# Layer 0 scan: which of the sixteen states' inputs ScalarE scales and TensorE turns, and which are made with diagonals of B

## The chip, the cores and the metric

The kernel runs on one core of a Trainium2 chip. The metric is the device time of one launch, in microseconds; it is given as the median of several runs. All four layers of the model are in this one launch. The change lies in layer 0 alone.

## What is computed

The model has four layers over an image tensor of shape (4, 48, 48, 128). Layer 0 is a two-dimensional selective state-space block. Cut to what matters here:

```python
# per image b, direction k (4: rows, columns, and both backwards), channel d (256), state n (16)
x_dbl = einsum('bkdl,kcd->bkcl', xs, x_proj_w)          # 8 dt rows, 16 B rows, 16 C rows
dt = softplus(einsum('bkrl,kdr->bkdl', dts_r, dt_proj_w) + dt_proj_b)
def step(h, inp):                                       # over the 2304 positions l
    dA = exp(dt_l[..., None] * A)
    h = h * dA + (dt_l * u_l)[..., None] * B_l[:, :, None, :]
    y = einsum('bkdn,bkn->bkd', h, C_l)
    return h, y
```

The result is the sum of the four directions, normalised, gated and projected. Layer 1 is a deformable convolution, layer 2 linear attention with experts, layer 3 causal attention and spectral filters; they are not touched.

## The kernel before

The scan of an image runs over the four directions, each cut into 6 pieces of 384 positions: 24 chunks per image, named g. Within a chunk it runs over the 16 states, so that there are 384 steps s with n = s % 16 and g = s // 16. Positions lie along the free axis, and the 256 channels are two halves of 128 partitions, which one scan instruction handles together.

For each step, the engines do this:

- ScalarE makes the decays exp(dt * A) with two instructions (`decays`, line 500), two steps ahead of the scan. There are four decay buffers.
- The input dt * u * B of the state is made in PSUM by `make_input` on TensorE, one step ahead of the scan, in one of two PSUM places. B varies along the positions, which are on the free axis, so it cannot be a per-partition factor there. There are two ways around it. A *straight* state uses `diagonal` on VectorE (line 556), which multiplies the identity with B to get three 128x128 diagonals, and six matmuls (line 408) of the turned dt * u with these. A *turned* state uses `turned_input` on ScalarE (line 490), which multiplies dt * u in its turned form by B as a per-partition scale, three instructions, and six transposes (line 406) back. `TURNED` lists the turned states. Diagonals are made two steps ahead and have three buffers; turned inputs are made three steps ahead and have two buffers (xT), so that one waits until the input of the turned state two before it has been made.
- VectorE scans (`scan`, line 579). A scan waits for its decays, its input and its carry.
- GpSimd multiplies the states with the C row (line 647) and then writes the carry columns for the step three ahead (`carry`, line 636, or a memset on line 634 in a direction's first chunk).
- TensorE turns the product and sums it over the states into y in PSUM (`sum_states`, line 419), three steps behind.

Beside this, in fixed slots of a chunk, the next chunk is projected (`project`). On TensorE: the rows of dt, B and C in slot 0 (line 361), the two halves of the dt projection in slots 2 and 5 (line 377), the turning of B in slot 8 (line 369) and of dt * u in slots 11 and 13 (line 389). ScalarE copies the rows in slot 1 (line 460), does the softplus in slots 3 and 6 (lines 470 to 474), and copies B and the turned dt * u later (lines 464 and 480). VectorE finishes dt after scans 4 and 7 (line 549). GpSimd multiplies dt * u after the product of state 7 (line 619). For directions 1 and 3 the rows and dt * u go through a view with x and y exchanged.

The finished y of a chunk is taken out of PSUM in the next one. In the first two directions ScalarE copies it, after the softplus of slot 3 (`keep_y`, line 506). In the other two VectorE adds it, after scan 2 (`add_y`, line 586). State 0 of the following chunk may be summed (S(0), the first of line 419 in a chunk) only after that.

Every engine works in the order that is written here. In step s TensorE does `make_input(s + 1)`, then `sum_states(s - 3)`, then `project`; ScalarE does `turned_input(s + 3)`, `decays(s + 2)`, `project`, `keep_y`; VectorE does `diagonal(s + 2)`, `scan(s)`, `project`, `add_y`. `make_input(s)` also waits until scan s - 2 has freed its PSUM place.

Of the kernel before, what the change touches and what calls it, by code (L numbers as in the profile page):

```python
# [70 lines left out]
NCS, NDC, NHC = 6, 4, 4  # L71
RX = 2 * RC + 6
X2_AT = BANK - RC - 4
TURNED = (2, 5, 7, 10, 12, 15)


def layer0(nc, x_in, w, x_out, c_rows):
    with ExitStack() as ctx:
# [107 lines left out]
        with nc.Fori(0, NB) as b:  # L186
# [107 lines left out]
            with nc.Block() as block:  # L294
# [13 lines left out]

                turned = [s for s in range(NSTEP) if s % NS in TURNED]
                straight = [s for s in range(NSTEP) if s % NS not in TURNED]  # L310
                rank = {s: i for own in (turned, straight) for i, s in enumerate(own)}
# [14 lines left out]
                def half(h):  # L326

                    return slice(2 + h * (RC + 2), 2 + h * (RC + 2) + RC)
# [26 lines left out]
                def _(pe):  # L355
# [36 lines left out]
                    def make_input(s):  # L392
                        n, g = s % NS, s // NS
                        if n == 0:
                            pe.wait_ge(s_tc, 2 * g + 2)
                        if n in TURNED:
                            pe.wait_ge(s_xT, rank[s] + 1)
# [4 lines left out]
                        for h in range(2):  # L402
                            for t in range(LB):
                                o = 2 * BANK * (s % 2) + X2_AT + half(h).start + t * P
                                if n in TURNED:
                                    mm = pe.transpose(ps[:, o:o + P], xT[:, rank[s] % 2, t, h * P:(h + 1) * P], ident[:])  # L406
# [46 lines left out]
                def _(act):  # L453
# [29 lines left out]
                    def turned_input(s):  # L483
                        n, g, i = s % NS, s // NS, rank[s]
                        act.wait_ge(s_bt, g + 1)
                        act.wait_ge(s_tc, 2 * g + 2)
                        if i >= 2:
                            act.wait_ge(s_x2, turned[i - 2] + 1)
                        for t in range(LB):
                            ins = act.activation(xT[:, i % 2, t, :], dtuT[:, g % 2, t, :], ACT.Copy, scale=BT[:, g % 2, t, n:n + 1])  # L490
                        ins.then_inc(s_xT, 1)
# [38 lines left out]
                    for s in range(3):  # L530
                        if s % NS in TURNED:
                            turned_input(s)
                    for s in range(NSTEP):
                        if s + 3 < NSTEP and (s + 3) % NS in TURNED:
                            turned_input(s + 3)
# [2161 lines left out]
```

## Time and profile before

| | us |
|---|---|
| median of 3 runs | 7712.57 |
| lowest and highest run | 7707.59, 7712.93 |
| span of the profiled execution | 7975.8 |
| TensorE busy in it | 7187.8 (90%) |
| VectorE busy | 5972.5 (75%) |
| ScalarE busy | 4078.3 (51%) |
| GpSimd busy | 3659.8 (46%) |

The profile is of one execution. Its span, from the first to the last instruction, is the only time known of that execution, and it is longer than the median. Layer 0 takes about the first half of it. The rows below are read so: an instruction's start and duration, then in square brackets how long its engine had been idle before it and what ended that. The durations of two neighbours on an engine can overlap, so the distance from start to start is what an instruction takes of its engine's queue.

### The profile page before, as it was taken

How to read it: one execution, taken by the hardware profiler on the slowest of the kernel's cores; microseconds unless marked ns; L12 is line 12 of the kernel's file. 1: busy time of each engine (PE TensorE's matmuls, PEld its weight loads, DVE VectorE, ACT ScalarE, POOL GpSimd, SP SyncE). 2: the span in 40 equal slices, each digit the busy share in tenths (PEclk: the TensorE clock that was granted, in tenths of full speed). 3: DMA queues.
4: the chain of work that ended last, by engine and by line, in shares of the span. 5: the costliest groups of instructions: out<-in, count | busy, mean ns of one | idle time of the engine just before them, and what ended most of it. 6: DMA issues, size and time to landing. Idle time of an engine off the chain costs nothing. (4 is left out here: it accounts for less than half of the span.)

```text
span 7975.8 us, 170513 instructions
## 1 busy us (share of the span) xinstructions
PE 7187.8 (90%) x62522; PEld 6186.6 (78%) x62522; DVE 5972.5 (75%) x9085; ACT 4078.3 (51%) x8541; POOL 3659.8 (46%) x4037
## 2 busy tenths in 40 slices
PE   8999899998999989999756788879988999999999
PEld 6888778886788867888546666645667989989999
DVE  7999889997899978999644555545556767767677
ACT  5888668885688757888311222224543222222222
POOL 5888658885688847888355555410000000000000
PEclk9999999999999999999878899889998999999999
DMA  2333223332233322333366555400003434434343
GB/s 66 90 93 93 75 64 92 93 90 68 74 90 93 92 58 83 90 94 90 109 174 171 164 160 152 119 4 3 0 6 95 125 116 125 125 116 128 113 129 108
DMA packets 590364, 763.42 MB, mean 96 GB/s; under 512 B 51703, under 2 KB 527896, under 8 KB 587585
## 3 DMA queue, kind: packets, MB, share of 16 engines
q1 hardware_dynamic: 537921, 585.72, 25.8%
q0 software_dynamic: 51840, 169.91, 7.5%
q8 instruction: 348, 5.70, 0.3%
q14 instruction: 255, 2.09, 0.1%
HBM read 721.77 MB, written 33.66 MB: 95 GB/s over the span
## 5 line engine op out<-in xcount | busy, mean ns | idle before, releaser
L647 POOL TENSOR_TENSOR l_arena<-l_arena 128x768 f32<-128x768 f32 x1536 | 2591.3, 1688 | 449.1 <-DVE l_arena L579 443.6
L579 DVE TENSOR_TENSOR_SCAN l_arena<-l_arena,psum 128x772 f32<-128x772 f32 x1536 | 2664.5, 1751 | 176.6 <-PE psum L406 72.5
L500 ACT ACTIVATE l_arena<-l_arena,l_A 128x384 f32<-128x384 f32 x3072 | 1643.7, 604 | 38.2 <-DVE l_arena L579 32.7
L408 PE MATMUL psum<-l_arena 128*128 128x128 f32 x11520 | 1499.3, 280 | 46.8 <-DVE l_arena L579 43.0
L408 PEld LDWEIGHTS psum<-l_arena 128*128 128x128 f32 x11520 | 1367.4, 192 | 170.5 <-issue 146.7
L419 PE MATMUL psum<-l_ident,l_arena 128*128 128x128 f32 x9216 | 1257.6, 273 | 50.6 <-ACT l_yT L506 41.7
L419 PEld LDWEIGHTS psum<-l_ident,l_arena 128*128 128x128 f32 x9216 | 1055.2, 141 | 60.2 <-POOL l_arena L647 60.2
L2269 POOL TENSOR_TENSOR st_mab<-st_xr 128x384 f32<-128x384 f32 x8 | 7.8, 1000 | 2053.1 <-DVE st_xr L2259 2053.1
L1211 POOL DMA_INDIRECT l_G<-neighbours,l_idx x648 | 621.2, 959 | 650.2 <-PE psum L1259 301.0
L490 ACT ACTIVATE l_arena<-l_arena,l_BT 128x256 f32<-128x256 f32 x1728 | 747.0, 496 | 7.5
L2544 ACT ACTIVATE st_own_s<-psum 128x384 f32<-128x384 f32 x256 | 125.7, 491 | 1092.5 <-PE psum L2381 1092.5
L1259 PE MATMUL psum<-l_ident,l_G 128*128 128x128 f32 x2592 | 361.8, 301 | 181.2 <-ACT l_val L1384 109.8
L2381 PE MATMUL psum<-st_FS,st_xt 128*128 128x128 f16 x6912 | 518.0, 219 | 4.4 <-DMA st_FS<-filter_sums 4.4
L556 DVE TENSOR_TENSOR l_arena<-psum,l_BT 128x384 f32<-128x384 f32 x960 | 510.8, 532 | 0.0
L1259 PEld LDWEIGHTS psum<-l_ident,l_G 128*128 128x128 f32 x2592 | 333.5, 157 | 212.6 <-issue 198.4
L406 PEld LDWEIGHTS psum<-l_ident,l_arena 128*128 128x128 f32 x3456 | 380.5, 140 | 143.8 <-issue 141.3
L406 PE MATMUL psum<-l_ident,l_arena 128*128 128x128 f32 x3456 | 486.9, 277 | 2.8 <-DVE l_arena L579 2.8
L2401 PE MATMUL psum<-st_Uc,st_Wm 128*128 128x128 f32 (+1 forms) x2560 | 448.6, 306 | 6.4 <-DVE st_Uc L2521 6.4
L2381 PEld LDWEIGHTS psum<-st_FS,st_xt 128*128 128x128 f16 x6912 | 434.7, 97 | 21.1 <-DMA st_FS<-filter_sums 4.8
L1054 DVE TENSOR_TENSOR l_G<-l_G,psum 128x1536 f32<-128x1536 f32 (+1 forms) x144 | 365.5, 2547 | 84.2 <-DMA l_G<-neighbours,l_idx 73.9
L2371 PE MATMUL psum<-st_F,st_xt 128*128 128x128 f16 x4608 | 427.4, 219 | 0.0
L2401 PEld LDWEIGHTS psum<-st_Uc,st_Wm 128*128 128x128 f32 x2560 | 351.4, 191 | 7.5 <-DVE st_Uc L2521 7.5
(436 smaller groups left out, 11291.5 us busy)
## 6 DMA issues: line engine op xcount, KB each, us to landing
l_arena<-c_rows SPq DMA_DIRECT2D x1536, 192.0 KB, 3.1
st_FS<-filter_sums SPq DMA_DIRECT2D x128, 1155.0 KB, 9.2
st_F<-filter_parts SPq DMA_DIRECT2D x128, 320.5 KB, 7.2
neighbours<-l_xt SPq DMA_DIRECT2D x256, 72.0 KB
st_mab<-in_st_mp SPq DMA_DIRECT2D x68, 256.0 KB, 9.5
st_mab<-in_st_mm SPq DMA_DIRECT2D x68, 256.0 KB, 6.2
l_G<-neighbours,l_idx POOLq DMA_INDIRECT x648
l_arena<-in_x SPq DMA_DIRECT2D x4, 1152.0 KB, 5.2
```

What stands on the lines that cost most here:

```text
L406: mm = pe.transpose(ps[:, o:o + P], xT[:, rank[s] % 2, t, h * P:(h + 1) * P], ident[:])
L408: mm = pe.matmul(ps[:, o:o + P], dtuT[:, g % 2, t, h * P:(h + 1) * P], diagB[:, rank[s] % 3, t, :], start=True, stop=True)
L419: mm = pe.matmul(y_ps[:, t, h * P:(h + 1) * P], hC[:, s % NHC, h, t * P:(t + 1) * P], ident[:], start=(n == 0 and h == 0 and t % 2 == 0), ...
L490: ins = act.activation(xT[:, i % 2, t, :], dtuT[:, g % 2, t, :], ACT.Copy, scale=BT[:, g % 2, t, n:n + 1])
L500: act.activation(decay[:, s % NDC, half(h)], dtv[:, g % 2, h, :], ACT.Exp, scale=A[:, g // NRC, h, n:n + 1]).then_inc(s_exp, 1)
L556: dve.tensor_tensor(diagB[:, i % 3], ident_ps.unsqueeze(1).broadcast_to([P, LB, P]), BT[:, g % 2, :, n:n + 1].broadcast_to([P, LB, P]), AL ...
L579: dve.tensor_tensor_scan(hbuf[:, n, run], decay[:, s % NDC, run], x2_ps[s % 2][:, run], 0.0, ALU.mult, ALU.add).then_inc(s_scan, 1)
L647: pool.tensor_tensor(hC[:, s % NHC], halves(hbuf[:, s % NS, :]), Cs[:, s % NCS, :].unsqueeze(1).broadcast_to([P, 2, RC]), ALU.mult).then_i ...
L1211: pool.indirect_dma_start(out=G[:, g, 4 * k:4 * k + 4, :].rearrange("p q c -> p (q c)"), out_offset=None, in_=tables[b], in_offset=bass.In ...
L1259: mm = pe.matmul(bank(i % 2, P * a, P * (a + 1)), G[:, g, 4 * k + q, :], ident[:], start=(q == 0), stop=(q == 3), is_transpose=True, skip_ ...
L2381: mm = pe.matmul(ps[:, at + i * P:at + (i + 1) * P], xt[:, xpart, x0 + LB - 1 - i, :], FS[:, r, fpart, z, three, shift + i * P:shift + (i ...
L2401: mm = pe.matmul(ps[:, o:o + hi - lo], Wm[:, r, z, m, :], src[:, lo - c * RC:hi - c * RC], start=False, stop=False, skip_group_check=True)
```

## The change

One line: the list of turned states goes from six to eight, and not by adding two. States 4, 8, 11 and 13 become turned, and 7 and 12 become straight; 2, 5, 10 and 15 stay turned.

```diff
@@ -71,7 +71,7 @@
 NCS, NDC, NHC = 6, 4, 4
 RX = 2 * RC + 6
 X2_AT = BANK - RC - 4
-TURNED = (2, 5, 7, 10, 12, 15)
+TURNED = (2, 4, 5, 8, 10, 11, 13, 15)
```

What this does to the order is seen on the engines. On TensorE, in a chunk from the first half of the dt projection (line 377) to the input of state 8; the rows of line 419 are the sums of states 0 to 3 of this chunk. Before:

```order
L377 MATMUL psum<-l_arena,l_dtp_w 128x384
L408 MATMUL psum<-l_arena 128x128 x6
L419 MATMUL psum<-l_ident,l_arena 128x128 x6
L406 MATMUL psum<-l_ident,l_arena 128x128 x6
L419 MATMUL psum<-l_ident,l_arena 128x128 x6
L408 MATMUL psum<-l_arena 128x128 x6
L419 MATMUL psum<-l_ident,l_arena 128x128 x6
L377 MATMUL psum<-l_arena,l_dtp_w 128x384
L406 MATMUL psum<-l_ident,l_arena 128x128 x6
L419 MATMUL psum<-l_ident,l_arena 128x128 x6
L408 MATMUL psum<-l_arena 128x128 x6
```

The same place on TensorE in the changed kernel:

```order
L377 MATMUL psum<-l_arena,l_dtp_w 128x384
L406 MATMUL psum<-l_ident,l_arena 128x128 x6
L419 MATMUL psum<-l_ident,l_arena 128x128 x6
L406 MATMUL psum<-l_ident,l_arena 128x128 x6
L419 MATMUL psum<-l_ident,l_arena 128x128 x6
L408 MATMUL psum<-l_arena 128x128 x6
L419 MATMUL psum<-l_ident,l_arena 128x128 x6
L377 MATMUL psum<-l_arena,l_dtp_w 128x384
L408 MATMUL psum<-l_arena 128x128 x6
L419 MATMUL psum<-l_ident,l_arena 128x128 x6
L406 MATMUL psum<-l_ident,l_arena 128x128 x6
```

The input of state 4, behind the first line 377, is now turned; that of state 7, behind the second, is now made with diagonals; that of state 8 is turned.

On VectorE, in a chunk from its second dt update (line 549, after scan 7) to scan 13. Before:

```order
L549 SCALAR_TENSOR_TENSOR l_arena<-psum,l_arena 128x384
L579 SCALAR_TENSOR_TENSOR l_arena<-l_arena,psum 128x772
L556 TENSOR_TENSOR l_arena<-psum,l_BT 128x384
L579 SCALAR_TENSOR_TENSOR l_arena<-l_arena,psum 128x772 x2
L556 TENSOR_TENSOR l_arena<-psum,l_BT 128x384
L579 SCALAR_TENSOR_TENSOR l_arena<-l_arena,psum 128x772
L556 TENSOR_TENSOR l_arena<-psum,l_BT 128x384
L579 SCALAR_TENSOR_TENSOR l_arena<-l_arena,psum 128x772 x2
```

The same place on VectorE in the changed kernel:

```order
L549 SCALAR_TENSOR_TENSOR l_arena<-psum,l_arena 128x384
L579 SCALAR_TENSOR_TENSOR l_arena<-l_arena,psum 128x772 x2
L556 TENSOR_TENSOR l_arena<-psum,l_BT 128x384
L579 SCALAR_TENSOR_TENSOR l_arena<-l_arena,psum 128x772 x2
L556 TENSOR_TENSOR l_arena<-psum,l_BT 128x384
L579 SCALAR_TENSOR_TENSOR l_arena<-l_arena,psum 128x772 x2
```

The diagonals of states 11 and 13 are gone and that of state 12 has come, before scan 10. Scans 8 and 9 now stand back to back.

## Rows read from the trace of the kernel before

**Rows 1.** The page's costliest groups: instruction, count, busy us, mean ns, idle before.

```profile
L408 PE MATMUL psum<-l_arena 128*128 128x128 f32 x11520 | 1499.3, 280 | 46.8 <-DVE l_arena L579 43.0
...
L490 ACT ACTIVATE l_arena<-l_arena,l_BT 128x256 f32<-128x256 f32 x1728 | 747.0, 496 | 7.5
...
L556 DVE TENSOR_TENSOR l_arena<-psum,l_BT 128x384 f32<-128x384 f32 x960 | 510.8, 532 | 0.0
...
L406 PE MATMUL psum<-l_ident,l_arena 128*128 128x128 f32 x3456 | 486.9, 277 | 2.8 <-DVE l_arena L579 2.8
```

**Rows 2.** Window of chunk 5: length, busy PE, PEld, DVE, ACT, POOL, granted clock, DMA.

```profile
268.47:304.07 35.60, 34.64 (x272) 29.88 (x270) 32.47 (x29) 28.85 (x62) 30.50 (x34) 1.00 0.33 90
```

**Rows 3.** Timeline of VectorE, chunk 10: start us, us, instruction, idle before.

```profile
446.75 1.76 DVE L579 TENSOR_TENSOR_SCAN l_arena<-l_arena,psum 128x772 f32<-128x772 f32 x1 [1.84 <-POOL l_arena L636]
...
451.78 1.76 DVE L579 TENSOR_TENSOR_SCAN l_arena<-l_arena,psum 128x772 f32<-128x772 f32 x1 [0.82 <-PE psum L408]
...
454.23 1.76 DVE L579 TENSOR_TENSOR_SCAN l_arena<-l_arena,psum 128x772 f32<-128x772 f32 x1 [0.24 <-ACT l_arena L500]
...
458.52 1.76 DVE L579 TENSOR_TENSOR_SCAN l_arena<-l_arena,psum 128x772 f32<-128x772 f32 x1
460.20 0.53 DVE L549 SCALAR_TENSOR_TENSOR l_arena<-psum,l_arena 128x384 f32<-128x384 f32 x1
...
466.09 0.53 DVE L556 TENSOR_TENSOR l_arena<-psum,l_BT 128x384 f32<-128x384 f32 x1
466.54 1.75 DVE L579 TENSOR_TENSOR_SCAN l_arena<-l_arena,psum 128x772 f32<-128x772 f32 x1
...
481.09 1.76 DVE L579 TENSOR_TENSOR_SCAN l_arena<-l_arena,psum 128x772 f32<-128x772 f32 x1 [0.58 <-PE psum L406]
```

**Rows 4.** Timeline of TensorE, start of chunk 10.

```profile
443.00 2.75 PE L361 MATMUL psum<-l_xc,l_xp_w 128*40 128x384 f32 x4
...
449.97 1.60 PE L408 MATMUL psum<-l_arena 128*128 128x128 f32 x12
452.52 0.85 PE L419 MATMUL psum<-l_ident,l_arena 128*128 128x128 f32 x6 [0.95 <-ACT l_yT L506]
...
456.60 0.91 PE L377 MATMUL psum<-l_arena,l_dtp_w 9*128 9x384 f32 x2
457.44 0.88 PE L406 MATMUL psum<-l_ident,l_arena 128*128 128x128 f32 x6
```

**Rows 5.** Timeline of ScalarE, start of chunk 10.

```profile
445.78 0.49 ACT L460 ACTIVATE l_arena<-psum 40x384 f32<-40x384 f32 x1 [3.53 <-PE psum L361]
446.17 1.30 ACT L490 ACTIVATE l_arena<-l_arena,l_BT 128x256 f32<-128x256 f32 x3
447.36 2.12 ACT L500 ACTIVATE l_arena<-l_arena,l_A 128x384 f32<-128x384 f32 x4
450.07 0.49 ACT L470 ACTIVATE l_arena<-psum 128x384 f32<-128x384 f32 x1 [0.58 <-PE psum L377]
```

**Rows 6.** Timeline of GpSimd, chunk 10, and one row of chunk 15.

```profile
460.36 1.69 POOL L647 TENSOR_TENSOR l_arena<-l_arena 128x768 f32<-128x768 f32 x1 [0.36 <-DVE l_arena L579]
...
462.13 2.39 POOL L619 TENSOR_TENSOR l_arena<-l_arena,l_xc 128x384 f32<-128x384 f32 x2
...
466.09 0.20 POOL L636 COPY l_arena<-l_arena 128x2 f32<-128x2 f32 x1
...
634.23 1.97 POOL L619 TENSOR_TENSOR l_arena<-l_arena,l_xc 128x384 f32<-128x384 f32 x2
```

**Rows 7.** Timeline of TensorE and VectorE, chunk 15: inputs 6, 7; scans 5, 7.

```profile
626.16 1.58 PE L408 MATMUL psum<-l_arena 128*128 128x128 f32 x12 [0.59 <-DVE l_arena L579]
...
629.16 0.87 PE L406 MATMUL psum<-l_ident,l_arena 128*128 128x128 f32 x6
...
626.38 1.75 DVE L579 TENSOR_TENSOR_SCAN l_arena<-l_arena,psum 128x772 f32<-128x772 f32 x1
...
630.62 1.75 DVE L579 TENSOR_TENSOR_SCAN l_arena<-l_arena,psum 128x772 f32<-128x772 f32 x1
```

## The prediction, made before the changed kernel ran

> **What bounds the kernel now.** I read the page's costliest groups first [rows 1]. The change touches three kinds of work in the layer 0 scan: the diagonals of B on VectorE (line 556), the B-scaled inputs on ScalarE (line 490) and TensorE's making of the scan input (lines 408 and 406). The window of one whole chunk [rows 2] says how full each engine is: in 35.60 us TensorE is busy 34.64, VectorE 32.47, ScalarE 28.85, GpSimd 30.50. No engine has much room, so busy time decides nothing. The timelines of one chunk [rows 3 to 6] have to be walked.
>
> I call the 24 runs of 16 states per image chunks 0 to 23. Chunk 10 is shown; its state 2 is scanned at 446.75 and that of chunk 11 at 481.09 [rows 3], and a chunk is measured here from its scan 2 to the next. I write x(n) for the input of state n in PSUM, and S(n) for the six transposes of line 419 that add state n to y. Three facts carry the argument.
>
> First, TensorE works in program order, and around the start of a chunk it, not VectorE, sets the pace. The row projection (2.75 us) runs from 443.00, and x(2) comes only after it [rows 4]. In chunk 10, S(0) starts at 452.52 after 0.95 us of idle that ScalarE's copy of y (line 506) ends. From there TensorE runs through x(5), S(1), x(6), S(2), the second dt projection at 456.60 and x(7) at 457.44 [rows 4].
>
> Second, the price of an input as the scan sees it. Straight (line 408, 12 instructions): x(4) starts at 449.97 and its scan at 451.78, so 1.81 us [rows 3, 4]. Turned (line 406, 6 instructions): x(7) starts at 457.44 and its scan at 458.52, so 1.08 us [rows 3, 4]. The difference is 0.73 us.
>
> Third, a diagonal costs VectorE 0.45 us of its queue, from 466.09 to the scan at 466.54 [rows 3]; the 0.53 of its own row overlaps the next instruction.
>
> **The change, part by part.** States 4, 8, 11 and 13 become turned, states 7 and 12 straight. Per chunk that is two diagonals fewer on VectorE (2 x 0.45 = 0.90 us), two more triples on ScalarE (2 x 1.20 = 2.4 us, by the 1.20 from 446.17 to 447.36 that one takes in the queue [rows 5]), and on TensorE 2 x 0.66 less. If all the VectorE saving reached the end, 96 chunks would give 86 us. It does not, state by state:
>
> State 4, turned. Its diagonal stood before scan 2, which waits 1.84 us for the projection [rows 3], or 0.58 in a chunk with the short one. So taking it away gains nothing. x(4) is ready 0.73 earlier, but S(0) behind it waits for the copy of y at 452.52, and that copy hangs on the first dt projection and the softplus on ScalarE, which do not move. So scan 5 stays at 454.23 and the gain of x(4) is lost. ScalarE's added triple for state 4 stands before the wait of 3.53 us at 445.78 and is hidden. The triple for state 5 must now wait until x(2) is made, at 446.17 + 0.4, because there are two xT buffers. That is covered by the 0.58 idle before 450.07 [rows 5]. If that cover were short, the dt softplus, the copy of y, S(0) and all behind them would be late.
>
> State 7, straight. This is the loss. x(7) starts at 457.44 as before, right behind the second dt projection, but takes 1.81 instead of 1.08. Scan 7 moves from 458.52 to 459.25: **+0.73**. The diagonals that move there (8 away before scan 6, 7 added before scan 5) are no help, since VectorE is waiting for TensorE: without the wait, scan 7 could start at about 458.3. This holds in the 12 chunks with the copy of y (1 to 12). In the chunks with the add of y on VectorE (13 to 22) TensorE waits 0.59 for scan 4 before x(6) at 626.16, x(7) starts at 629.16 and its scan at 630.62 [rows 7]. It becomes 629.16 + 1.81 = 630.97: **+0.35**.
>
> States 8, 11, 13 turned and 12 straight, from scan 7 on. VectorE sets the pace there, and between scans 7 and 15 it loses diagonals 11 and 13 and gains 12: **-0.45**. x(9) stays straight with one diagonal less around it. It is ready 0.23 + 1.81 = 2.04 us after scan 7 ends (0.23 from scan 4's end at 625.93, the start 626.38 of [rows 7] less 0.45, to 626.16), against 2.12 that the dt update and scan 8 take. So it fits, with 0.08 to spare.
>
> GpSimd, untouched, is late next. Scan n needs the carry that GpSimd writes after the product of state n-3. After scan 7 its queue holds delta x u (line 619): 2.39 us in chunks 5 to 10 and 17 to 22, where it writes through a turned view, 1.97 in the others [rows 6]. The carry for scan 11 ends at 466.29, 6.09 us after scan 7's end at 460.20. Scan 11 started 6.34 after, and now would start 5.89 after [rows 3, 6]. The trace shows no wait of VectorE on GpSimd that is certain; the way over is between 0 (466.29 itself) and 0.25 (since 6.34 was no wait). ScalarE to TensorE and VectorE to GpSimd take 0.05 to 0.2 (460.20 to 460.36 [rows 3, 6]), so I take 0.1. That gives 6.19 - 5.89 = **+0.30**, with bounds 0.20 and 0.45, in those 12 chunks; in the short ones 0.4 us less, thus nothing (at most 0.06).
>
> The Trainium skill has a rule against this reading. "Perfetto Trace Analysis", section Identifying the Most-Contended Engine, says that the engine with the highest occupancy is to be relieved first, and that TensorE's room is to be judged by LDWEIGHTS busy time, not by matmul busy time. By that rule VectorE is the bound, with 32.47 us against 29.88 of weight loads [rows 2], and the whole VectorE saving would arrive. The rows above disagree at the start of a chunk, where VectorE idles.
>
> **The sum**, per image: 12 chunks x (0.73 - 0.45) = +3.4; 10 chunks x (0.35 - 0.45) = -1.0; GpSimd 12 x 0.30 = +3.6; chunk 0, which has neither copy nor add of y, about -0.25 and chunk 23, which projects nothing and is held by straight inputs and the last add, about -0.1. Together +5.6 us, over four images **+22 us**. Against the profiled span that is 7975.8 to 7998. The span is 263 us (3.4%) above the median of 7712.57, and nothing shows where. The terms are lengths of queued instructions at a granted clock of 1.00 [rows 2], so I carry them over unchanged: 7735 us, 0.29% slower. With GpSimd's bounds: 12 x 4 x 0.20 = 9.6 to 12 x 4 x 0.45 = 21.6, plus 2.4 for the short chunks, in place of 14.4. The sum is then 18 to 32, time 7730 to 7745.
>
> **The rivals.**
>
> A. VectorE is the bound throughout, the whole 0.90 us per chunk arrives: 7712.6 - 86 = 7626. For it: VectorE is busy 32.47 of 35.60, and for most of a chunk its rows are back to back. Against it: the waits before scans 2, 4 and 5 [rows 3]. This is also what the skill's rule would give.
>
> B, the other side. TensorE catches up before x(7), so that straight 7 costs nothing, and only diagonals 11 and 13 less 12 count, -0.45 in every chunk: -43. With GpSimd's 14 it is 7684. It is decided by whether x(7) starts before about 456.5 in chunk 10; that takes S(0) about 0.9 earlier than 452.52. For it: x(4) ends 0.7 earlier. Against it: the wait that holds S(0) ended with line 506, not with TensorE.
>
> C. Both signs cancel, since unprofiled waits are shorter than profiled ones: the loss at scan 7 shrinks to about half (0.37 and 0.18), and per image that is 12 x (-0.08) - 10 x 0.27 + 3.6 - 0.35 = -0.4. Time about 7711, band 7697 to 7727.
>
> D. ScalarE is late in the copy of y. The cover is 0.58 - 0.4 = 0.18 us. If a triple that waits costs 0.4 more than I took, 12 x 4 x 0.4 = 19 us come on top: 7754; with late inputs for 8, 10, 11 too, up to 7770. For it: 2.4 us more on an engine of 28.85. Against it: it idles 3.53, 0.58 and more in each chunk [rows 5].
>
> **How the numbers follow.** Forecast 0.58, A 0.04, B 0.14, C 0.13, D 0.11. The predicted time is the forecast's, 7735. Left out are A and B with 0.18; the range then runs from C's lower end to just under D's upper one: 7697 to 7765. A difference under 0.2%, 15.4 us, is about what a measurement of this kernel cannot tell from none. Faster by more: A and B, 0.18. Within: C and the thin lower edge of the forecast, 0.16. Slower: 0.66.
>
> **What would show each step.** In the changed trace: scan 7 of chunk 10 waits for line 408 and starts 3.0 us after scan 6, where it was 2.2; scan 5 stays 7.48 us behind scan 2; scan 4 comes 0.7 earlier; the idle before S(0) grows from 0.95 to about 1.7; scan 11 has a wait on line 636 of about 0.3 in chunks 5 to 10 and 17 to 22, and none elsewhere. Chunk 10 gets about 0.6 longer (34.34 to 34.9), one like chunk 2 about 0.3 longer, one like 15 0.1 shorter. Line 556 has 768 instructions, line 490 has 2304. I am wrong if scan 7 does not wait for TensorE, or if the copy of y moves.

## The result, and the profile after

| | before | after |
|---|---|---|
| median, us | 7712.75 | 7791.76 |
| lowest and highest of 4 runs each | 7707.59, 7713.07 | 7790.40, 7796.82 |
| span of the profiled execution | 7975.8 | 7790.3 |
| first and last statistics of layer 0 (line 196), start us | 15.6, 2949.0 | 15.5, 3006.0 |

The ratio is 1.0109, with a 95% interval from 1.0094 to 1.0123: 1.1% slower, 79 us. The forecast was 7735, the range 7697 to 7765. The sign was right, the size was not: of 79 us only 22 had been foreseen.

The page of the changed kernel, its span, the busy times, the granted clock in 40 slices, and the groups that answer to [rows 1]:

```profile
span 7790.3 us, 168593 instructions
...
PE 7053.1 (91%) x61370; PEld 6041.7 (78%) x61370; DVE 5897.6 (76%) x8893; ACT 4312.5 (55%) x9117; POOL 3655.8 (47%) x4037
...
L408 PE MATMUL psum<-l_arena 128*128 128x128 f32 x9216 | 1212.5, 282 | 116.4 <-DVE l_arena L579 95.4
...
L490 ACT ACTIVATE l_arena<-l_arena,l_BT 128x256 f32<-128x256 f32 x2304 | 997.3, 496 | 56.6 <-PE psum L406 49.1
...
L406 PE MATMUL psum<-l_ident,l_arena 128*128 128x128 f32 x4608 | 668.8, 283 | 24.3 <-DVE l_arena L579 23.7
...
L556 DVE TENSOR_TENSOR l_arena<-psum,l_BT 128x384 f32<-128x384 f32 x768 | 409.2, 533 | 0.0
```

The work moved as the diff says: 192 diagonals fewer, 576 scalings more, 1152 transposes more, 2304 straight matmuls fewer. VectorE's busy time fell by 75 us, TensorE's by 135, and the kernel is 79 us slower. The line for 406 has its mean up from 277 [rows 1] to 283 ns. A transpose has no reason to take longer, so the clock has to be looked at. That comes below.

The profiled span of before is not a guide to the result. Of the 263 us by which it exceeds the median, 255 lay in layer 1, as the gathers of its line 1211 show, first in the trace of before, then of after (count, ns min/median/max, first and last start):

```profile
L1211 POOL DMA_INDIRECT l_G<-neighbours,l_idx x648: 943/949/2733, 4006.7 to 5131.9; - x162
```

```profile
L1211 POOL DMA_INDIRECT l_G<-neighbours,l_idx x648: 942/949/2792, 4082.1 to 4952.0; - x162
```

They took 1125 us in that one execution of before and 870 in after. When they start, after is 75 us behind. So nearly the whole loss is in layer 0, and there the profile of before is a sound base.

### The profile page after: what moved, and what is told of

Same layout as the page of the kernel before. It is cut to its first block and busy times, and to the rows that moved or that the text cites. A ratio compares the mean times of both kernels' runs of the same rounds, so it can differ in the third digit from the quotient of the medians.

```text
span 7790.3 us, 168593 instructions
## 1 busy us (share of the span) xinstructions
PE 7053.1 (91%) x61370; PEld 6041.7 (78%) x61370; DVE 5897.6 (76%) x8893; ACT 4312.5 (55%) x9117; POOL 3655.8 (47%) x4037
## 3 DMA queue, kind: packets, MB, share of 16 engines
q1 hardware_dynamic: 537921, 585.72, 25.6%
## 5 line engine op out<-in xcount | busy, mean ns | idle before, releaser
L419 PE MATMUL psum<-l_ident,l_arena 128*128 128x128 f32 x9216 | 1290.2, 277 | 87.4 <-ACT l_yT L506 80.4
L408 PE MATMUL psum<-l_arena 128*128 128x128 f32 x9216 | 1212.5, 282 | 116.4 <-DVE l_arena L579 95.4
L408 PEld LDWEIGHTS psum<-l_arena 128*128 128x128 f32 x9216 | 1100.3, 193 | 258.4 <-issue 245.6
L419 PEld LDWEIGHTS psum<-l_ident,l_arena 128*128 128x128 f32 x9216 | 1082.5, 144 | 100.2 <-POOL l_arena L647 97.4
L490 ACT ACTIVATE l_arena<-l_arena,l_BT 128x256 f32<-128x256 f32 x2304 | 997.3, 496 | 56.6 <-PE psum L406 49.1
L406 PE MATMUL psum<-l_ident,l_arena 128*128 128x128 f32 x4608 | 668.8, 283 | 24.3 <-DVE l_arena L579 23.7
L406 PEld LDWEIGHTS psum<-l_ident,l_arena 128*128 128x128 f32 x4608 | 529.0, 144 | 174.7 <-issue 167.9
L556 DVE TENSOR_TENSOR l_arena<-psum,l_BT 128x384 f32<-128x384 f32 x768 | 409.2, 533 | 0.0
L1259 PE MATMUL psum<-l_ident,l_G 128*128 128x128 f32 x2592 | 314.8, 281 | 69.9 <-DVE l_G L1054 41.8
L1259 PEld LDWEIGHTS psum<-l_ident,l_G 128*128 128x128 f32 x2592 | 299.5, 145 | 92.4 <-DVE l_G L1054 47.9
```

What stands on the lines that cost most here:

```text
L408: mm = pe.matmul(ps[:, o:o + P], dtuT[:, g % 2, t, h * P:(h + 1) * P], diagB[:, rank[s] % 3, t, :], start=True, stop=True)
L419: mm = pe.matmul(y_ps[:, t, h * P:(h + 1) * P], hC[:, s % NHC, h, t * P:(t + 1) * P], ident[:], start=(n == 0 and h == 0 and t % 2 == 0), ...
L1259: mm = pe.matmul(bank(i % 2, P * a, P * (a + 1)), G[:, g, 4 * k + q, :], ident[:], start=(q == 0), stop=(q == 3), is_transpose=True, skip_ ...
```

## Where the 79 us are: one chunk length at a time

VectorE's second dt update (line 549, after scan 7) comes once in a chunk. The distance from one to the next, worked out from the starts of line 549 in the traces, is the length of a chunk, and from an image's first to its last is called its scan block here. The first image:

| us, from chunk to chunk | 1 to 2 | 3 to 4 | 6 to 7 | 8 to 9 | 10 to 11 | 16 to 17 | 19 to 20 |
|---|---|---|---|---|---|---|---|
| before | 34.34 | 34.33 | 35.89 | 35.60 | 34.33 | 35.65 | 35.65 |
| after | 34.61 | 36.53 | 37.72 | 37.65 | 36.61 | 35.56 | 35.90 |
| after, with transposes in the gap (`e5_fill`, below) | 34.61 | 34.88 | 36.03 | 36.18 | 34.93 | 35.56 | 35.89 |

The scan blocks of the four images sum to 3181.4 us before and 3259.3 after: +77.8, which is the result but for about 1 us. Some chunks behave as forecast (1 to 2: +0.27, forecast +0.28; 16 to 17: -0.09, forecast -0.10). The chunks into 4 to 11, in the later images 1 as well, are 1.4 to 1.7 us longer on top of that.

In such a chunk, chunk 9 of the changed kernel, VectorE's timeline reads so (start us, us, instruction, idle before and what ended it):

```profile
421.78 1.76 DVE L579 TENSOR_TENSOR_SCAN l_arena<-l_arena,psum 128x772 f32<-128x772 f32 x1 [2.29 <-POOL l_arena L636]
...
426.08 1.76 DVE L579 TENSOR_TENSOR_SCAN l_arena<-l_arena,psum 128x772 f32<-128x772 f32 x1
427.76 0.53 DVE L549 SCALAR_TENSOR_TENSOR l_arena<-psum,l_arena 128x384 f32<-128x384 f32 x1
...
430.55 1.76 DVE L579 TENSOR_TENSOR_SCAN l_arena<-l_arena,psum 128x772 f32<-128x772 f32 x1 [1.79 <-PE psum L406]
432.69 1.76 DVE L579 TENSOR_TENSOR_SCAN l_arena<-l_arena,psum 128x772 f32<-128x772 f32 x1 [0.38 <-PE psum L408]
...
435.72 1.76 DVE L579 TENSOR_TENSOR_SCAN l_arena<-l_arena,psum 128x772 f32<-128x772 f32 x1 [0.82 <-PE psum L408]
437.39 0.53 DVE L549 SCALAR_TENSOR_TENSOR l_arena<-psum,l_arena 128x384 f32<-128x384 f32 x1
...
443.61 1.76 DVE L579 TENSOR_TENSOR_SCAN l_arena<-l_arena,psum 128x772 f32<-128x772 f32 x1 [0.24 <-POOL l_arena L636]
```

Scan 4 comes 4.30 us behind scan 2, against 5.03 before [rows 3], so the gain of x(4) is there. Scan 5 then waits 1.79 us for its transposes and comes 8.77 behind scan 2, where 7.48 was forecast and measured before. Scan 7 comes 3.03 behind scan 6, with a wait of 0.82 for line 408, as forecast. Why x(5) is late stands on TensorE, in the same chunk:

```profile
424.16 0.91 PE L377 MATMUL psum<-l_arena,l_dtp_w 9*128 9x384 f32 x2
425.00 0.87 PE L406 MATMUL psum<-l_ident,l_arena 128*128 128x128 f32 x6
427.55 1.51 PE L419 MATMUL psum<-l_ident,l_arena 128*128 128x128 f32 x6 [1.68 <-ACT l_yT L506]
428.86 1.49 PE L406 MATMUL psum<-l_ident,l_arena 128*128 128x128 f32 x6
430.13 1.01 PE L419 MATMUL psum<-l_ident,l_arena 128*128 128x128 f32 x6
430.98 1.50 PE L408 MATMUL psum<-l_arena 128*128 128x128 f32 x12
```

x(4) is done early, and TensorE then idles 1.68 us for the copy of y, not 0.95 [rows 4]. The six transposes S(0) behind it take 1.51 us in place of 0.85, and those of x(5) 1.49. The windows of these stretches show what TensorE's clock did (length, busy PE, PEld, DVE, ACT, POOL, granted clock, DMA share, GB/s):

```profile
420.70:425.80 5.10, 5.10 (x39) 4.22 (x38) 3.78 (x3) 4.48 (x10) 3.00 (x5) 1.00 0.27 85
425.80:427.55 1.75, 0.07 (x2) 0.03 (x1) 1.66 (x2) 1.72 (x4) 1.63 (x2) 0.87 0.29 94
427.55:428.86 1.31, 1.31 (x7) 1.31 (x8) 1.20 (x3) 1.31 (x4) 0.00 (x0) 0.50 0.33 67
428.86:430.13 1.27, 1.27 (x7) 1.27 (x7) 0.00 (x0) 1.27 (x4) 0.89 (x1) 0.50 0.55 109
430.13:430.98 0.85, 0.85 (x7) 0.85 (x7) 0.43 (x1) 0.85 (x2) 0.85 (x2) 0.77 0.08 23
430.98:433.90 2.92, 2.92 (x22) 2.21 (x20) 2.54 (x2) 0.65 (x2) 1.58 (x2) 1.00 0.20 67
```

The granted clock was 1.00, fell during this idle, stood at 0.50, which is 1.2 of 2.4 GHz, for S(0) and x(5), and came back during S(1). Over 92 to 930 us it was 1.00 before and is 0.98 after:

```profile
92.00:930.00 838.00, 813.86 (x6423) 713.84 (x6422) 784.58 (x695) 677.56 (x1435) 730.46 (x816) 1.00 0.32 91
```

```profile
92.00:930.00 838.00, 783.61 (x6000) 677.10 (x6000) 751.00 (x637) 723.51 (x1557) 711.96 (x800) 0.98 0.30 90
```

In 35 of the 48 chunks with a copy of y the clock falls (8 in the first image, 9 in each other): there the distance from the first to the second dt update is 9.57 to 9.87 us, in the other 13 it is 8.19 or 8.20. Those 13 have the same idle. In chunk 2 of the changed kernel, TensorE's row for S(0) and the windows of the idle and of what follows read:

```profile
169.34 0.84 PE L419 MATMUL psum<-l_ident,l_arena 128*128 128x128 f32 x6 [1.68 <-ACT l_yT L506]
```

```profile
165.80:169.30 3.50, 1.86 (x10) 0.93 (x8) 3.41 (x3) 3.36 (x8) 3.24 (x4) 1.00 0.33 102
169.30:170.70 1.40, 1.36 (x13) 1.40 (x14) 1.24 (x3) 1.40 (x4) 0.34 (x1) 1.00 0.26 88
```

So the longer idle makes a fall possible and does not force it. The Trainium skill tells of a like case in "TensorE: Matmul & The Clock Gate", section A second HAM failure mode: psum-queue depth-cycling: short idles between groups of matmuls, not one long stop, let the clock go back and forth between its two levels. The trace agrees, with 0.50 behind 1.68 us of idle.

## The experiments

The theory after the trace: turning state 4 lengthens TensorE's idle ahead of S(0) by 0.73 us, the clock falls at it, and that is some 57 of the 79 us; the terms of the forecast are the rest. The rivals: the loss is from the fuller ScalarE, or from state 7 and GpSimd at more than their price, and the clock only shows it; or the clock falls because TensorE has less to do in the whole chunk, and not because of this one idle. The runs were made in three sets, each with runs of before on the same chip: e1, e2 and e4 against 7709.6 us, e5 to e8 against 7708.9, e9 and e10 against 7704.94.

| label | turned states, other edit | us | ratio to before, 95% interval |
|---|---|---|---|
| e2_four_straight | 2, 5, 8, 10, 11, 13, 15 | 7725.25 | 1.0020 (1.0010 to 1.0029) |
| e1_four_only | 2, 4, 5, 7, 10, 12, 15 | 7734.48 | 1.0030 (1.0019 to 1.0042) |
| e4_seven_for_four | 2, 5, 7, 8, 10, 11, 13, 15 | 7665.29 | 0.9942 (0.9926 to 0.9959) |
| e5_fill | as after, 12 more transposes in the idle | 7726.85 | 1.0025 (1.0014 to 1.0036) |
| e7_after_copy_first | as after, copy of y ahead of the softplus | 7661.07 | 0.9935 (0.9918 to 0.9951) |
| e6_best_copy_first | as e4, copy of y ahead of the softplus | 7627.78 | 0.9893 (0.9877 to 0.9910) |
| e8_split_du | as e6, dt * u of GpSimd in two parts | 7617.85 | 0.9883 (0.9866 to 0.9899) |
| e10_before_copy_first | as before, copy of y ahead of the softplus | 7681.27 | 0.9969 (0.9956 to 0.9982) |
| e9_nine | as e8, and 4 | 7615.90 | 0.9882 (0.9864 to 0.9900) |

### State 4 straight again

```diff
-TURNED = (2, 4, 5, 8, 10, 11, 13, 15)
+TURNED = (2, 5, 8, 10, 11, 13, 15)
```

> The changed kernel with state 4 straight again (turned: 2, 5, 8, 10, 11, 13, 15). Clock theory: in the changed kernel, turning state 4 lengthens TensorE's idle before S(0) from 0.95 to 1.68 us, and the granted clock falls to half there in 8 or 9 of the 12 chunks with the copy of y. With state 4 straight the idle is 0.95 again and the clock stays full, while straight state 7 still costs 0.73 and 0.35. Sum per image: 12 x 0.28 - 10 x 0.1 + 12 x 0.2 - 0.3 = 4.5 us, so 7731 us (7722 to 7740). Rival, ScalarE theory: the loss comes from the extra ScalarE work or its order in the other states; then it stays near 7780 (over 7760). Rival, state 7 is dearer than thought: also near 7780, with full clock.

Measured 7725.25: 16 us over its own before, where after is 79 over, so 63 us are back. TensorE at S(0), chunk 9 of this kernel:

```profile
420.43 0.85 PE L419 MATMUL psum<-l_ident,l_arena 128*128 128x128 f32 x6 [0.95 <-ACT l_yT L506]
```

The idle is 0.95 again, S(0) takes 0.85 in all 48 chunks, and the two dt updates are 7.47 or 7.48 us apart in each. With a straight state more, and so more work on VectorE and TensorE, the kernel is faster than after. The four scan blocks sum to 3207.0, 25.6 more than before, though the median is only 16 more. In the profiled executions the rest of layer 0, outside the scan blocks, differs by up to 15 us with no edit there (in this one it is 9 us shorter than in before), so that blocks and medians need not agree to 10 us.

### State 4 turned, and nothing else

```diff
-TURNED = (2, 5, 7, 10, 12, 15)
+TURNED = (2, 4, 5, 7, 10, 12, 15)
```

This one stands against the kernel before: the diff and the times compare with it.

> The kernel before with state 4 turned and nothing else changed (turned: 2, 4, 5, 7, 10, 12, 15). Clock theory: the idle before S(0) is 1.68 us and the clock falls behind it in many of the 12 chunks with the copy of y; each fall costs about 1.6 us at scan 7, so with 8 or 9 of 12 chunks about 7769 us (7740 to 7790). Rival: the idle itself is harmless, and only together with straight state 7 is there a loss; then 7712 (7705 to 7720).

Measured 7734.48, 25 us slower than before: the rival's 7712 is out, and the 7769 of the theory is missed as well. Chunks 9 and 10 of this kernel at S(0), TensorE:

```profile
424.46 0.85 PE L419 MATMUL psum<-l_ident,l_arena 128*128 128x128 f32 x6 [1.67 <-ACT l_yT L506]
...
460.05 1.51 PE L419 MATMUL psum<-l_ident,l_arena 128*128 128x128 f32 x6 [1.68 <-ACT l_yT L506]
```

The idle is 1.67 or 1.68 in every chunk, and the clock fell in six of twelve per image. Where it did not fall, most chunks have their length of before (34.33 from 3 to 4, 35.60 from 8 to 9), which is what the forecast said of the gain of x(4): nothing gained, nothing lost. Two of them, each right behind a chunk with a fall, are 0.3 us longer. Where it fell, a chunk is 1.4 to 1.7 us longer. The mechanism stands; how often it strikes was assumed to be as in after and is not. Which chunks fall is not explained by the idle. The scan blocks sum to 3217.9, 36.5 over those of before; the profiled execution was the slowest of seven, and the median is 25 over.

### The idle filled

Between x(4) and S(0) TensorE makes x(5) twice more, in the place where x(5) is made anyway, so that no value changes and 12 transposes are added in each of the 12 chunks. The two waits are those that x(5) has in any case.

```diff
                         make_input(s + 1)
+                        if s % NS == 3 and 1 <= s // NS <= 2 * NRC:
+                            pe.wait_ge(s_xT, rank[s + 2] + 1)
+                            pe.wait_ge(s_scan, s + 1)
+                            for _ in range(2):
+                                for h in range(2):
+                                    for t in range(LB):
+                                        o = 2 * BANK * (s % 2) + X2_AT + half(h).start + t * P
+                                        pe.transpose(ps[:, o:o + P], xT[:, rank[s + 2] % 2, t, h * P:(h + 1) * P], ident[:])
```

> The changed kernel, but TensorE makes the input of state 5 two extra times (12 transposes, 12 x 0.109 = 1.3 us) between the input of state 4 and S(0) in the 12 chunks with the copy of y. That fills most of the 1.68 us idle and moves nothing else. Clock theory: the granted clock stays at 1.00, the scans keep their places, 7725 us as with state 4 straight (7717 to 7735). Rival, the loss comes from ScalarE's order or load, the extra work is only extra: 7792 or more.

Measured 7726.85, 18 us over its own before against 79: 61 us are back, with more work. TensorE in chunk 9; its line numbers from 452 on are 8 higher, so that 514 is the copy of y and 452 are the added transposes:

```profile
417.07 0.88 PE L406 MATMUL psum<-l_ident,l_arena 128*128 128x128 f32 x6
417.79 1.48 PE L452 MATMUL psum<-l_ident,l_arena 128*128 128x128 f32 x12
419.63 0.84 PE L419 MATMUL psum<-l_ident,l_arena 128*128 128x128 f32 x6 [0.36 <-ACT l_yT L514]
420.31 0.82 PE L406 MATMUL psum<-l_ident,l_arena 128*128 128x128 f32 x6
```

And the windows of the filled stretch and of the one behind it:

```profile
417.00:419.63 2.63, 2.27 (x20) 1.96 (x19) 2.54 (x3) 2.49 (x6) 2.32 (x4) 1.00 0.21 63
419.63:421.20 1.57, 1.57 (x15) 1.57 (x16) 1.20 (x3) 1.57 (x5) 0.55 (x1) 1.00 0.42 83
```

S(0) still starts when the copy of y is done; only the idle is gone, and with it the fall, in all 48 chunks (8.20 or 8.21 between the dt updates). ScalarE's load, state 7 and GpSimd are as in after, so these rivals are out. The scan blocks sum to 3204.4: 54.9 us less than after, over 35 chunks 1.57 us for each fall. The other 23 us (3204.4 less 3181.4; 18 in the medians) stand where the forecast had 22.

The Trainium skill, "TensorE: Matmul & The Clock Gate", section Part 4: PE-mode transpose, says that the full clock does not engage for transposes. By that the fill would have done nothing. Here 12 transposes in the idle kept the clock at 1.00; the measurement decides.

### State 7 turned in place of state 4

```diff
-TURNED = (2, 4, 5, 8, 10, 11, 13, 15)
+TURNED = (2, 5, 7, 8, 10, 11, 13, 15)
```

> State 4 straight and state 7 turned, the rest as in the changed kernel (turned: 2, 5, 7, 8, 10, 11, 13, 15; eight again). Both causes of loss are away. Theory: against the kernel before, -0.45 in the 12 chunks with the copy of y (diagonals 11 and 13 less 12), -0.83 in the 10 with the add (diagonal 8 counts too there, up to x(7)'s readiness), +0.2 for GpSimd in 12 chunks: -11.8 us per image, -47 in all, 7665 us (7655 to 7685). Difference to the run with state 4 straight and 7 straight: 12 x 0.73 + 10 x 0.73 = 16 us per image, 64 in all. Rival, ScalarE is too full for eight: over 7700.

Measured 7665.29, as expected. Against e2, which differs by state 7 alone, that is 60 us. A chunk is 0.73 us shorter, with the copy (34.61 to 33.88) and with the add (34.30 to 33.57). The forecast's 0.35 for the chunks with the add was a price against the kernel before, in which VectorE still makes the diagonal of state 8 there. The dt updates are 6.74 apart in chunks with the copy and 5.98 with the add. The idle ahead of S(0) is 0.95 and the clock does not fall in any chunk, although TensorE has exactly as much to do as in after. So it is not the amount of its work that brings the fall.

### The copy of y ahead of the softplus

In ScalarE's slot 3 (only the lines that move are shown):

```diff
+                        g = s // NS - 1
+                        if s % NS == 3 and 0 <= g < 2 * NRC:
+                            keep_y(g)
                         if s // NS + 1 < NCH:
                             project(s // NS + 1, s % NS)
-                        g = s // NS - 1
-                        if s % NS == 3 and 0 <= g < 2 * NRC:
-                            keep_y(g)
```

First in the changed kernel, with 4 turned and 7 straight:

> The changed kernel with ScalarE's copy of y ahead of the softplus of slot 3 instead of behind it. Theory (the copy of y holds S(0), and the wait for it lets the clock fall): S(0) starts right behind x(4), about 1.7 us earlier, no idle, no fall. The chunks with the copy then behave as those with the add did: x(7) about 0.85 earlier in its straight form. Scan 7 at about -0.1 against the kernel before, -0.45 after it: 12 x (-0.55) - 1.0 + 2.0 - 0.3 = -5.9 us per image, 7686 us (7675 to 7705). Rival, TensorE's order after S(0) is bound otherwise: about 7725, only the clock's loss back.

Measured 7661.07, 25 us better than expected. TensorE and then ScalarE at S(0) of a chunk of this kernel:

```profile
437.50 0.88 PE L406 MATMUL psum<-l_ident,l_arena 128*128 128x128 f32 x6
438.37 0.85 PE L419 MATMUL psum<-l_ident,l_arena 128*128 128x128 f32 x6
```

```profile
437.44 0.79 ACT L506 ACTIVATE l_yT<-psum 128x768 f32<-128x768 f32 x1
438.13 0.47 ACT L470 ACTIVATE l_arena<-psum 128x384 f32<-128x384 f32 x1
```

S(0) now starts 0.87 us behind x(4), with no idle of note. Scan 7 comes 11.00 us behind scan 2 (11.77 in before, 13.94 in the chunk of after above). S(0) starts 1.7 us earlier than before, as expected. But the expectation let only 0.85 us of that reach x(7), as in the chunks with the add, and put scan 7 at 0.1 us earlier than before. In fact x(7) starts 9.20 us behind scan 2, where it was 10.69: 1.49 earlier, and scan 7 is 0.77 earlier. The idle of 0.95 and the 0.73 us of x(4), which had been lost to the wait, nearly all arrive. The clock does not fall in any chunk, with the same work on TensorE as in after.

Then with state 7 turned and 4 straight:

> Turned states 2, 5, 7, 8, 10, 11, 13, 15 (7 in place of 4) with the copy of y ahead of the softplus. Theory: scan 7 comes about 0.75 earlier in 12 chunks than without the move: 7665 - 36 = 7629 us (7620 to 7645). Rival, VectorE's first dt update gets late by the 0.7 us that the softplus moves back: no gain, 7665.

Measured 7627.78, as expected.

And the same move in the kernel before, without any other edit:

> The kernel before (turned 2, 5, 7, 10, 12, 15) with only the copy of y moved ahead of the softplus. It tells what the move gives by itself. Theory: S(0) comes 1.1 us earlier in 12 chunks, x(7) is ready in time, and scans 5 to 7 are then held by VectorE and by x(4): about 0.4 us per chunk with the copy, 12 x 4 x 0.4 = 19 us, 7690 us (7680 to 7698). Rival: the move only helps where state 7 is straight or the clock falls; 7709.

Measured 7681.27, 9 us less than expected. The chunks with a copy are 0.40 us shorter, as expected, and one of them 0.69; the scan blocks sum to 20 us less. The order in which ScalarE does its two things in slot 3 cost the kernel before 24 us.

### GpSimd's product of dt and u in two parts

One half after the product of state 7, the other after that of state 8, on top of e6. The diff is cut to the calls; the helper itself is changed to make the half that it is given.

```diff
-                            delta_u(s // NS + 1)
+                            delta_u(s // NS + 1, (0,))
+                        if s % NS == 8 and s // NS + 1 < NCH:
+                            delta_u(s // NS + 1, (1,))
```

> As the run before in this set, and GpSimd's delta x u in two halves, the first after the product of state 7, the second after that of state 8 and its carry. Theory (the carry for state 11 makes scan 11 wait 0.2 us in the 12 chunks with the slow form): 10 us less than without the split, 7620 us. Rival, another carry is then late, or turning dt x u gets late: no gain or a loss.

Measured 7617.85, 10 us less than e6. Most long chunks lose 0.24 us (34.72 to 34.48, 35.16 to 34.92), and the short ones nothing. That is the wait of scan 11 on line 636, 0.24 in the timeline of chunk 9 above.

### Nine turned states

```diff
-TURNED = (2, 5, 7, 8, 10, 11, 13, 15)
+TURNED = (2, 4, 5, 7, 8, 10, 11, 13, 15)
```

This stands on top of e8.

> Nine turned states (2, 4, 5, 7, 8, 10, 11, 13, 15), copy of y first, delta x u in two halves. Theory: x(4) is 0.73 earlier in the 12 chunks with the copy, where scan 4 waits 0.82 for it: 12 x 4 x 0.7 = 34 us less than 7618, 7584 us (7575 to 7600). Rival, ScalarE (28.85 + 3 x 1.2 = 32.5 us of a period of 33 to 34.5) becomes the bound: decays or inputs late, 7618 or more.

Measured 7615.90: no gain beyond e8 that can be told, where 34 us had been expected. The window of e9 over most of an image:

```profile
92.00:930.00 838.00, 792.09 (x6081) 676.02 (x6081) 773.03 (x647) 761.95 (x1656) 729.57 (x816) 0.99 0.31 92
```

ScalarE is busy 762 of 838 us, where it was 731 in e8. The clock's 0.99 is from the first us of the window, ahead of chunk 1; in the chunks with a copy it does not fall. In the crowded part of a chunk it is late with the second softplus and then with decays, as VectorE and ScalarE show in chunk 3 of e9:

```profile
207.70 0.56 DVE L549 SCALAR_TENSOR_TENSOR l_arena<-psum,l_arena 128x384 f32<-128x384 f32 x1 [0.35 <-ACT l_arena L474]
208.18 3.55 DVE L579 TENSOR_TENSOR_SCAN l_arena<-l_arena,psum 128x772 f32<-128x772 f32 x2
```

```profile
208.77 1.11 ACT L500 ACTIVATE l_arena<-l_arena,l_A 128x384 f32<-128x384 f32 x2
```

Behind scan 2, scans 4 and 7 come 0.73 us earlier than in e8 (4.29 and 10.28 in place of 5.02 and 11.01), so state 4 does give its 0.73 once the wait for the copy has gone. The dt updates are then 6.41 us apart in place of 5.99, and 0.42 is taken back. Scan 9 starts at 209.97, right behind the decays that end at 209.88, and scan 10 at 212.18 likewise; behind scan 2 they are only 0.14 and 0.04 us earlier than in e8. So all of the gain is lost beside waits on ScalarE. This is what the forecast's rival D feared, ScalarE too full, at nine turned states and not at eight, and in the softplus and the decays, not in the copy of y.

## Why the prediction was wrong, point by point

**What bounds the start of a chunk.** Right. TensorE in program order sets scans 4 to 7; relieving VectorE there gave nothing. Rivals A and B needed the opposite, and are out: 192 diagonals fewer did not shorten one chunk with a copy of y, and scan 7 came 0.73 us later behind scan 2 also where the clock did not fall (12.49 in chunk 2, 11.76 before).

**State 4, the step that failed.** The text said that S(0) waits for the copy of y, that scan 5 stays, "and the gain of x(4) is lost". It foresaw the idle ahead of S(0) growing from 0.95 to about 1.7, and 1.68 was measured. It priced that idle at nothing. The sum had been built on "lengths of queued instructions at a granted clock of 1.00", a clock read in a trace where the idle was 0.95. The edit lengthens the idle, and with it this premise no longer held: the clock fell to 0.50 at the idle in 35 of 48 chunks. The missing term is 35 chunks x 1.57 = 55 us in the trace, some 60 in the medians. Two kernels show it from both sides: 63 us come back when the idle is shortened (e2), 61 when it is filled (e5). No rival weighed it either: none had a loss behind a longer idle of TensorE.

**State 7, straight.** Right. 3.03 us from scan 6 to scan 7 with a wait on line 408, forecast 3.0; turning it in e2's set of states gives 60 us (e4).

**States 8, 11, 12, 13.** Right. Chunks without a fall and with the short product of GpSimd are 0.27 longer with the copy (forecast 0.28), 0.09 shorter with the add (0.10).

**GpSimd's carry.** Nearly right. The forecast wait of scan 11 was 0.30 us, with bounds of 0.20 and 0.45. The row has 0.24 (443.61 above). By the chunk lengths of e5, less those of before and less 0.28, it is 0.30 to 0.34 in chunks 5 and 7 to 10. Chunk 6, 0.29 longer than its neighbours already in before (35.89), comes out 0.14 below the forecast's length without a wait, and the chunk from 3 to 4, which was said to have none, gets 0.27. The same reading with the add gives 0.34, 0.16, 0.33, 0.33 and 0.07 for chunks 17 to 21. The misses nearly cancel in the first half of an image, and in the second they leave 1.2 us where 1.5 had been forecast.

**The sum.** Without the clock it holds: e5, which is the changed kernel with the clock kept up, has scan blocks 23 us above before in the trace and a median 18 us above, against +22. That it comes so close is in part luck, as the misses on GpSimd's carry show. The prediction of 7735 was that of a kernel whose clock does not move.

**ScalarE (rival D).** The triple for state 5 waits 0.40 us for x(2), exactly as reckoned, and the softplus starts without idle behind it; the copy of y did not move. ScalarE in chunk 9 of after:

```profile
421.70 1.30 ACT L490 ACTIVATE l_arena<-l_arena,l_BT 128x256 f32<-128x256 f32 x3 [0.40 <-PE psum L406]
...
425.11 0.49 ACT L470 ACTIVATE l_arena<-psum 128x384 f32<-128x384 f32 x1
...
426.61 0.79 ACT L506 ACTIVATE l_yT<-psum 128x768 f32<-128x768 f32 x1
```

D gave 7754 to 7770 by a mechanism that did not occur: that it lies nearest to the measured time is no merit. Rival C, that unprofiled waits are shorter, is out too: the medians moved as the traces did.

**The range.** Its upper end was set by D alone. The trace of before had no row of TensorE behind an idle of more than 0.95 in this loop, and what the text did for GpSimd's carry, to set a bound on either side of what the trace does not show, it did not do for the clock.

## What to carry to other kernels

Before an edit makes an instruction shorter that stands ahead of a fixed wait of TensorE, read the granted clock behind that wait: a gain that ends in a longer idle can come back as a loss, since what follows may run at half the clock. Move or shorten what is waited for (here one copy, put ahead of a softplus, gave 24 us alone and about 130 in the changed kernel, about half of it the clock's), or give TensorE something harmless to do meanwhile. Then ask again which states to turn: by slot, not by number, since eight turned states gave 7791 or 7665 us by which eight they were, and a ninth gave nothing once ScalarE was full.

## What the runs showed of the hardware that was not expected

- TensorE's granted clock fell from 1.00 to 0.50 at an idle of 1.68 us, ahead of which it had been busy without a gap for 5.10 us at 1.00 (chunk 9 of after), and stood at 0.50 for some 2.6 us of transposes. With an idle of 0.95 us (e2, e4) or 0.36 us (e5) at the same place it never fell, in 48 chunks each.
- The same idle of 1.68 us was followed by a fall in 35 of 48 chunks of one kernel, and in 24 of 48 in another (e1), in nearly the same chunks in each image. What tells them apart stays open; no run was made for it.
- Twelve fp32 transposes in the idle kept the clock at 1.00 in all 48 chunks (e5).
